# GNN layer on Trainium2: VectorE computes block, chunk and places of its next marking in registers behind the fourth edge dot instead of just in front of the marking

## The reference, cut to what matters

```python
dst = minimum((6250 * uniform((200000,)) ** 2.0).astype(int32), 49999)     # then sorted
h = relu(layernorm(x))
scores = sum(q[dst] * k[src], -1) * 256 ** -0.5 + edge_weight * we + be
attn = softmax of scores over the edges of each dst
out = segment_sum(v[src] * attn, dst)
y = layernorm(h + out + linear(h, ws, bs)) ; y = layernorm(y + ffn(y)) ; result x + y
```

## Time and profile before

| | us |
|---|---|
| median of 3 runs | 2417.12 (2415.76 to 2421.07) |
| the profiled execution: its own time | 2417.61 |
| its span | 2415.7 |
| busy: TensorE | 2220.9 (92%) |
| busy: VectorE | 1748.0 (72%) |
| busy: GpSimd | 1628.4 (67%) |
| busy: ScalarE | 1166.5 (48%) |

### The profile page before, as it was taken

The page is one execution under the profiler, slowest core; times in us unless marked ns, Lnnn a source line. Parts: engine busy times, 40 slices in busy tenths (PEclk is TensorE's granted clock), DMA queues, the critical chain, the costliest instruction groups (busy, mean ns, idle before and its releaser), DMA issues. The chain is left out here.

```text
span 2415.7 us, 69601 instructions
## 1 busy us (share of the span) xinstructions
PE 2220.9 (92%) x14709; PEld 1858.0 (77%) x14710; DVE 1748.0 (72%) x7374; ACT 1166.5 (48%) x2875; POOL 1628.4 (67%) x1817
## 2 busy tenths in 40 slices
PE   5779989999999999999999999999999999989994
PEld 4568777777777777777888888888888888877883
DVE  6767767676777777777777777777777777784367
ACT  5545444444444444444444554455545454454454
POOL 3557777777777777777777777777777777302355
PEclk9889999999999999999999999999999999999997
DMA  7434444444444444444444444444444444240024
GB/s 236 131 96 146 139 137 137 138 136 138 138 139 137 137 137 139 137 137 140 137 139 137 139 137 139 137 139 137 139 137 139 137 130 137 72 137 4 0 63 141
DMA packets 148690, 311.05 MB, mean 129 GB/s; under 512 B 34127, under 2 KB 85186, under 8 KB 148665
## 3 DMA queue, kind: packets, MB, share of 16 engines
q0 software_dynamic: 75264, 205.62, 29.4%
q1 hardware_dynamic: 55278, 90.19, 11.6%
q10 hardware_dynamic: 18122, 14.96, 2.0%
HBM read 290.21 MB, written 20.43 MB: 129 GB/s over the span
## 5 line engine op out<-in xcount | busy, mean ns | idle before, releaser
L788 POOL DMA_INDIRECT work<-h_rows,idx x1536 | 1455.9, 948 | 482.8 <-issue 443.1
L876 PE MATMUL bank<-work 128*128 x3520 | 836.0, 380 | 0.0
L813 PE MATMUL bank<-q,onehot 128*128 x5304 | 739.0, 274 | 31.1 <-DVE work L961 21.3
L961 DVE SCALAR_TENSOR_TENSOR work<-bank,work 128x257 bf16<-128x257 f32 x1764 | 647.0, 425 | 98.6 <-SPq L752 86.4
L876 PEld LDWEIGHTS bank<-work 128*128 128x128 f32 x3520 | 634.2, 190 | 78.7
L813 PEld LDWEIGHTS bank<-q,onehot 128*128 128x128 bf16 x5304 | 513.7, 98 | 105.6 <-issue 43.8
L920 ACT ACTIVATE work<-work 128x1 f32<-128x1 f32 x440 | 129.6, 295 | 722.8 <-DVE work L1018 722.8
L924 ACT COPY work<-bank 128x256 f32<-128x256 f32 x880 | 285.5, 377 | 306.7 <-PE bank L863 306.6
L950 DVE TENSOR_SCALAR onehot<-dst_words,node 128x512 bf16 x443 | 173.6, 392 | 262.8 <-issue 198.2
L1018 DVE CUSTOM_DVE_ANT_0 work<-bank,work 128x512 f32<-128x512 f32 x440 | 328.8, 747 | 43.0 <-issue 22.8
L863 PE MATMUL bank<-ident,work 128*128 128x128 f32 x1760 | 277.0, 280 | 64.9 <-ACT work L921 63.8
(11 more groups left out here) (190 smaller groups left out, 1573.1 us busy)
## 6 DMA issues: line engine op xcount, KB each, us to landing
dst_words<-dst_short SPq DMA_DIRECT2D x99, 512.0 KB
work<-h_rows,idx POOLq DMA_INDIRECT x1568
bias<-h_rows ACTq DMA_DIRECT2D x56, 128.0 KB
r_rows<-bias ACTq DMA_DIRECT2D x55, 128.0 KB
work<-r_rows SPq DMA_DIRECT2D x49, 128.0 KB, 2.1
acc<-in_x SPq DMA_DIRECT2D x4, 1536.0 KB, 15.5
h_rows<-acc SPq DMA_DIRECT2D x12, 512.0 KB, 4.4
work<-in_x SPq DMA_DIRECT2D x48, 128.0 KB, 2.1
```

What stands on the lines that cost most here:

```text
L788: pool.indirect_dma_start(rows[:, u, j, 0:D], None, h_rows, bass.IndirectOffsetOnAxis(idx[:, half, u * J + j:u * J + j + 1], 0)).then_inc( ...
L813: last = nc.tensor.matmul(banks[j][:, 0:D1], onehot[:, k, j, :], q3[:, bass.ds(b, 1), c, 0:D1], start=(c == 0), stop=(c == 2))
L876: last = nc.tensor.matmul(banks[6 + k][:, 0:D1], probs[:, j, :], rows[:, bass.ds(slot, 1), j, :], start=(j == 2), stop=(j == 1))
L961: last = nc.vector.scalar_tensor_tensor(out=product[:, j, 0:D1], in0=banks[j][:, 0:D1], scalar=SCALE, in1=rows[:, bass.ds(slot, 1), j, :], ...
```

## The change

Block, chunk, the threshold of the DMA wait and the place in `dst_of` are computed by a function of their own, `place_of_mark`, and `mark` takes them ready. In steps u = 0 to 6 it is called in `meanwhile`, behind the fourth dot, together with `block_at(u)` and `block_at(u + 1)`. In u = 7 `meanwhile` loads the table as before, and the place is computed in front of the marking as before. The threshold `s + 2` of the wait for `outside_done` is computed at the head of the step.

```diff
-                def mark(step, b, k):
+                def place_of_mark(step):
                     chunk = chunk_of(dve, step)
                     there = dve.to_reg((chunk >> 2) * 16 + 16)
+                    at = dve.snap(dve.to_reg((chunk & (G - 1)) * C), min_val=0, max_val=(G - 1) * C)
+                    return there, at, block_of(dve, step)
+
+                def mark(place, k):
+                    there, at, b = place
                     dve.wait_ge(dst_in, there)
-                    nc.vector.tensor_scalar(onehot[:, k], dst_of[:, bass.ds((chunk & (G - 1)) * C, C)].rearrange("p (j n) -> p j n", j=J), node[:, bass.ds(b, 1)], None, ALU.is_equal).then_inc(onehot_done, 1)
+                    nc.vector.tensor_scalar(onehot[:, k], dst_of[:, bass.ds(at, C)].rearrange("p (j n) -> p j n", j=J), node[:, bass.ds(b, 1)], None, ALU.is_equal).then_inc(onehot_done, 1)
...
+                        place, after_next = {}, dve.to_reg(s + 2)
+
+                        def meanwhile():
+                            if to_next:
+                                load_steps(i + 1)
+                            else:
+                                place[0] = place_of_mark(step_at(regs[u + 3]))
+                                block_at(u)
+                                block_at(u + 1)
...
-                        edge_scores(step_at(regs[u + 1]), r, s + 1, 1 - k, (lambda: load_steps(i + 1)) if to_next else None)
+                        edge_scores(step_at(regs[u + 1]), r, s + 1, 1 - k, meanwhile)
...
-                        next_mark = step_at(regs[u + 3 - U if to_next else u + 3])
-                        blocks[u + 3] = block_of(dve, next_mark)
-                        dve.wait_ge(outside_done, s + 2)
-                        mark(next_mark, blocks[u + 3], 1 - k)
+                        if to_next:
+                            place[0] = place_of_mark(step_at(regs[u + 3 - U]))
+                        blocks[u + 3] = place[0][2]
+                        dve.wait_ge(outside_done, after_next)
+                        mark(place[0], 1 - k)
```

More of the change, by code:

```diff
@@ L985, in _ @@
                 dve.sem_inc(onehot_done, S)
-                mark(ahead[0], blocks[0], 0)
-                mark(ahead[1], blocks[1], 1)
+                mark(place_of_mark(ahead[0]), 0)
+                mark(place_of_mark(ahead[1]), 1)
                 read_max(0, 0, blocks[0])
@@ L990, in _ @@
                 dve.wait_ge(outside_done, 1)
-                mark(ahead[2], blocks[2], 0)
+                mark(place_of_mark(ahead[2]), 0)
                 dve.wait_ge(sums_set, 2)
```

## The result

The changed kernel takes 2410.5 us (median of 15 runs, 2406.3 to 2415.1) beside 2418.7 us of the kernel before in 15 runs on the same occasion (2415.6 to 2422.3). The ratio, that of the means, is 0.9969, 95% interval 0.9961 to 0.9976: **7.5 us faster** (5.8 to 9.4); the medians lie 8.2 us apart. That is over the 0.2% that a measurement can tell, and little more than half of the 13.9 us forecast; the time of 2410.5 us lies inside the range, near its upper end.

What follows compares the result with a forecast made beforehand. GpSimd's gathers bound the first 60% of the loop, then the consumers fall behind. Cutting the debt from 19.6 to 5.7 us gains 13.9 us: 2417.1 to 2403.2 us, range 2397.5 to 2411.5 (forecast's own 2401 to 2408).

Steps and rivals of the forecast that it cites:

- the debt: How late the consumers end the loop behind GpSimd's gathers: 19.6 us before the change, 5.7 us forecast after it.
- the end of the gathers: GpSimd's gathers, untouched by the change, were to keep their pace and still end at 2077 us.
- rule for TensorE's stall: At the border of two trips: step time minus 3.95 minus 0.35 us slack, 0.38 us of stall in u = 7.
- T: Consumers' mean time per step late in the loop: 4.30 us before, 4.16 forecast, range 4.13 to 4.21.
- wrong in the whole, if the gathers' pace moves: Sign that the whole prediction fails: GpSimd's pace, 1.254 us a gather all through the loop, changes.
- The cover: Running time of VectorE's fourth dot, about 1.0 us, was to hide the moved block of about 0.6 us.
- Who follows whom: Consumers follow GpSimd's gathers early in the loop, then fall behind; waits seen to about 1800 us instead of 1310.
- What is late next: TensorE, 3.95 us a step, holds a trip to at least 32.8 us; an ordinary step keeps 0.03 of 0.49 us.
- Rival B: Only 0.2 of the 0.6 us before the marking goes: T 4.25, gain 6.0 us, 2411 us; chance 0.16.
- C: No change: marking's idle time stays or compiler undoes the move; T 4.28 or more, gain below 3 us; chance 0.09.
- D: Slower: the block outgrows its cover, from 1.5 us; at 1.6 us 15 us lost, 2432 us; chance 0.05.
- A: TensorE's floor is reached late in the loop: T 4.10, gain 17.6 us, 2399.5 us; chance 0.15.

Runs made afterwards that it cites:

- i4: h1 with each marking cut to the first of its four groups of 128 edges: 0.9965 of the kernel before.
- h1: The changed kernel with bounds on VectorE's threshold registers and 62 never-executed instructions ahead of the loop: 2418.4 us, 0.9991 of the kernel before.
- j3: h1 with the marking moved behind the addition of sums: 0.9994 of the kernel before.
- i1: The kernel before with the same bounds and unexecuted instructions as h1, no block moved: 1.0056 of the kernel before.
- j2: i1 with q expanded from one of its three parts, two thirds of the expansion's matmuls left out: 1.0023 of the kernel before.
- i3: h1 with the block behind the fourth dot in u = 7 too, ahead of the table's loads: 0.9995 of the kernel before.
- j1: h1 with q expanded from one of its three parts, two thirds of the expansion's matmuls left out: 0.9964 of the kernel before.
- f1: The kernel before with bounds and 62 never-executed instructions ahead of the loop: 1.0017 of the kernel before, which took 3282 us on that occasion.

## Where the prediction was wrong, and what of it was right

Two steps of the prediction failed: the debt was sized too small, and the end of the gathers, which the sum held fixed, moved. The rest of the mechanism came as written. TensorE at the border, kernel after: the step from 2002.24 is u = 7, that from 2006.72 is u = 0.

```profile
2002.24 0.60 PE L863 MATMUL bank<-ident,work 128*128 128x128 f32 x4
...
2006.72 0.66 PE L863 MATMUL bank<-ident,work 128*128 128x128 f32 x4 [0.37 <-ACT work L921]
...
2010.85 0.60 PE L863 MATMUL bank<-ident,work 128*128 128x128 f32 x4
```

- **The step that sized the debt.** I took u = 7, 4.68 us from mask to mask, as something "which the change leaves". It takes 4.83 in every late trip, since the idle time in front of its marking grew from 0.57 to 0.73 us. The prediction's own rule for TensorE's stall gives with it 4.83 - 3.95 - 0.35 = 0.53 us in place of 0.38, and TensorE's rows agree. From L863 to L863 the steps u = 0 to 7 of late trips take 4.12, 3.95, 4.17, 3.95, 3.94, 4.91, 3.94 and 4.48 us: the transposes (u = 2) and the projection (u = 5) cost what I took, the stall in u = 7 is 0.53, and u = 0 adds 0.17 in place of 0.11. The trip is 33.46 us in place of 33.3, T = 4.18 in place of 4.16. The formula squares what is left of the loop, so these 0.02 us raise the debt from 5.7 to 0.82 * 0.00032 * 4.18 * (391 - 310)², 7.2 us. Measured: 8.3. **The debt was mis-sized by 2.6 us**, of which the formula explains 1.5; the other 1.1 stays open.
- **"Gathers still end at 2077 us".** I wrote that the change touches nothing of GpSimd, and put this term at nothing. They end at 2081.7. 2.4 us of it is that the 1536 gathers took longer, from first to last, and this the change makes, as i4 and the table of gathers show: it puts markings over them. My own sign "wrong in the whole, if the gathers' pace moves" stood there; it moved by 2.4 in 1927 us, which took a sixth of the forecast gain. The other 2.4 us, the later start, lies ahead of the gathers. In the nine kernels from h1 to j3 the first gather starts at 151.7 to 155.6 us, in the two with the order of before (i1, j2) at 151.9 and 155.6: I take it for chance, which is argued and not shown.
- **The sum**, from the two profiled executions: 13.9 - 2.6 - 2.4 - 2.4 + 1.8 (a shorter tail) = 8.3, against 8.4 between the two spans. The ratio over all runs says 7.5. The later start and the shorter tail nearly cancel, and that is luck. That 2410.5 us lies inside the range is owed to the width taken for the rivals: the forecast's own range ended at 2408.
- **The cover** was right. L956 starts as L1038 ends in the ordinary step, L973 comes no later than before, and L1038 to L956 saved all 0.59 us in it (0.49 forecast, up to 0.59). In u = 0, with two block numbers more, L973 waits 0.30 us where 0.21 or less is usual: 0.1 us stands out, as forecast. i3 shows the cover's end: with the loads beside the block 0.88 us stand out.
- **Who follows whom** was right. The waits for L752 reach up to 1754 us (1800 forecast) and are 115 us more on the page; the late waits are for L819. They are there 78 times in 180 steps, not in most.
- **What is late next** was right: TensorE. j1 shows it for the changed kernel, and j2 that it wasn't so before, both with the bounds.
- **Rival B** has the time, 2411 us, but not the mechanism: all of the 0.6 us went, T is 4.18 and not 4.25. Rivals C and D are ruled out by the rows above, A by the trip of 33.46.

## What to carry to other kernels

An engine's saving counts only in the steps where no other engine is late next: list the period of each unrolled step, not their mean, and look first at the steps behind the loop's border. Where consumers fall behind a constant producer only towards the end, the end's gain goes by the square of what is left of the loop, so 0.02 us in a step is 1.5 us at the end; give the range accordingly. Look also at the step that keeps the old order: here, where it calls the same function as the moved steps, its block became 0.15 us longer. And a consumer that catches up walks in step with its producer: ask whether their instructions then fall on each other.

## What the hardware showed that I had not expected

- Markings of 0.36 us on VectorE that begin 1.0 to 1.2 us behind a gather's start on GpSimd make the next gather 0.99 to 1.00 us long instead of 0.947; cut to 0.25 us they don't (0.950). Begun 0.4 to 0.6 us behind a gather's start they take 0.46 to 0.49 us themselves.
- A loop body with 359 in place of 321 records of VectorE in a trip made each of 55 returns cost 3 to 5 us (288 instruction packets in place of 17) and the kernel 6% slower. With 345 records, and 62 instructions ahead of the loop that move it, nothing was loaded in the trips (18 packets). Length and place weren't varied one at a time.
- On three occasions every kernel took 3276 to 3400 us, with long waits of ScalarE for a signal of no named sender (735 us of them in f1), and no gain of the change could be measured there. The cause stays open.
